# First stage of an audio tower: chunks of 512 and 480 tokens, another order of the seven products, the first norm folded into the second

## The chip, the cores and the metric

The kernel runs on one core of one Trainium2 chip. The metric is the device time of one execution in microseconds (us). Lower is better.

## The reference

```python
# x: 32 x 750 x 320, padded to 752 rows and reshaped to 32 x 94 tokens of 2560
x = rms_norm(x, ln_pre_w)                   # eps 1e-6
h = x @ w1.T                                # 1024 columns
h = silu(h[..., 512:]) * h[..., :512]
h = rms_norm(h @ w2.T, ln_post_w)           # 1024 columns, eps 1e-6
h = h + attention(layernorm(h), ...)        # 32 heads, 94 tokens per batch
h = h + ffn_with_lora(layernorm(h), ...)    # 1024 columns, 8 experts
```

All inputs and outputs are float32. There are 32 x 94 = 3008 tokens. The change is in the first four lines of arithmetic.

## The kernel before

The kernel has five parts, one behind the other: `tok_up` (w1 and the gate), `tok_down` (w2, the second norm, and products of weights for the attention), `attention`, `attn_out` and `ffn`. An fp32 product is made of three matmuls of rounded halves: each operand is split into a high half (ScalarE copies it into the rounded type) and a low half (VectorE subtracts the high half from the operand).

`tok_up` computes C = w1 x transposed: 1024 rows by 3008 tokens over 2560 inputs. It uses a scheme of seven products instead of eight: w1 and x are cut in two by two blocks, some products take a sum or difference of two blocks, and each result is added to, subtracted from or written to one or two blocks of C. `SEVEN` lists for each product the blocks of w1 (`a`), the blocks of x (`b`) and where the result goes (`into`; SET writes, NEG writes the negative, ADD adds, SUB_ subtracts, FROM writes block (0, n) less the result). The tokens are cut into six chunks (`TOKC`), two of which (one of either half) make a pair. The loop runs over 7 products x 3 pairs x 10 blocks of 128 inputs, 210 steps; ten steps with one product and pair are a group, and group(i, pr) is number 3 i + pr. A step has 4 row blocks of 3 matmuls each. The results of a group stay in four PSUM banks, and two sets of banks alternate.

For each step, SP loads one or two blocks of x (six slots `raw`, so up to three sums ahead); GpSimd adds or subtracts the two (L517, two buffers, each free when the low half of the step two sums back is made); ScalarE makes the high half (L575, five buffers t, each free when TensorE has used it); VectorE makes the low half (L668). TensorE waits for the low half (L756 is the first of the three matmuls, L758 the last). So the makers can run at most some four steps ahead of TensorE. The weights go the same way: ScalarE scales a block by the first norm's weight (L546); where the product takes a sum GpSimd adds two (L503) and ScalarE copies the high half (L558); VectorE makes the low half (L618, L621). `FILL` says at which steps of the product before, and of pair 0 of the same product (written as pair 3), the weights of a product are begun.

The first norm's factor is one number per token. During products 0 to 3 ScalarE squares each x block (L590), and the squares are added to `ssq` by VectorE (L678) where the step is a sum, and otherwise by GpSimd (L529); pair 1 of product 3 is also GpSimd's. In group(4, 1) TensorE sums `ssq` over partitions by 24 matmuls of one column in a row (L732), VectorE turns the sums into factors (L684, `inv_sqrt_wide`) and into diagonal matrices (L651), two per `RATE_AT` group. TensorE spreads them over all partitions with a matrix of ones (L739) into banks that the group itself needs for its row blocks 2 and 3, and ScalarE copies them to `ssq` (L599, L600) four steps later in its own order. VectorE then multiplies the gate half of C by the factor (L699), ScalarE takes silu, VectorE multiplies by the factor again (L703) and multiplies the value half by the gate half (L708). SP stores the result g to DRAM. VectorE evicts a group's four banks in steps 5 to 8 of the next (L639 for SET, L645 for ADD).

The last `NT` = 5 steps are done row block by row block (L770 to L772), so that VectorE can evict the first block while TensorE does the next; the last chunk's g is made and stored in four parts (L714, L495). SP waits for all stores, the stage ends, and `tok_down` loads g again in 24 tiles of 128 tokens (L904), splits w2 (L222, L229), splits g (L1027, L1124), multiplies by w2 (L244), and takes mean square, root and a Newton step for the second norm (L1059, L1149). Beside this it centres `wa` (L1235, L1109, L1001) and folds weights of the attention (L1218, L1226, L1247). Its first tiles are done by peeled code, the rest in a loop over six tiles.

## Time and profile before

| what | value |
|---|---|
| median of 3 runs | 2511.26 us (2506.93 to 2512.43) |
| profiled execution | 2511.18 us, span 2509.5 us |
| TensorE busy | 2377.4 us, 95% of the span |
| VectorE, ScalarE, GpSimd busy | 1815.0, 1246.3, 1231.2 us |
| mean granted clock of TensorE | 0.974 |
| `tok_up` | up to about 635 us |
| `tok_down` | about 635 to 960 us |

Busy time counts an engine's instructions from start to end; PE is TensorE, PEld its loads of weights, DVE VectorE, ACT ScalarE, POOL GpSimd, SP SyncE, which here only issues DMAs. The granted clock is a share of full speed, so 1.00 is 2.4 GHz and 0.50 is 1.2 GHz.

### The profile page before, as it was taken

The numbers are of one execution on the slowest core, as the hardware profiler recorded it, in microseconds if no ns is written. First come the engines' busy times: TensorE is split into PE (matmuls) and PEld (weight loads), VectorE is DVE, ScalarE is ACT, GpSimd is POOL, SyncE is SP. The second block draws the span as 40 slices with busy tenths as digits, with TensorE's granted clock in tenths as the row PEclk, the third lists the DMA queues.
The fourth block names the chain that finished last, engine by engine and source line by source line (L and its number), as shares of the span: only waits on it lengthen the run. The fifth ranks groups of instructions, "written<-read, shape, count | busy, mean of one in ns | idle before, by whom it ended". The sixth has DMA issues, their size and how long they took to land. (4 is left out here: it accounts for less than half of the span.)

```text
span 2509.5 us, 45975 instructions
## 1 busy us (share of the span) xinstructions
PE 2377.4 (95%) x14716; PEld 2061.9 (82%) x14716; DVE 1815.0 (72%) x3545; ACT 1246.3 (50%) x3736; POOL 1231.2 (49%) x1017
## 2 busy tenths in 40 slices
PE   8999999988699996999999999999999996999998
PEld 7888878776466676999999999878888885999998
DVE  8875586795446666898889898855776566777775
ACT  5664454442334545999999999922222222111110
POOL 5774675774013225677677767620676553111110
PEclk9999999999899998999999999989999998999999
DMA  7654576667556651111111111287788996211111
GB/s 251 209 175 127 183 258 226 214 227 265 165 170 198 198 188 59 48 43 56 50 55 45 51 56 54 70 284 225 213 252 244 284 288 224 71 68 68 67 67 51
DMA packets 318257, 379.44 MB, mean 151 GB/s; under 512 B 25472, under 2 KB 260480, under 8 KB 317952
## 3 DMA queue, kind: packets, MB, share of 16 engines
q1 hardware_dynamic: 310320, 349.67, 44.3%
q0 software_dynamic: 7184, 25.69, 2.6%
q10 hardware_dynamic: 576, 2.10, 0.3%
q8 instruction: 65, 1.06, 0.2%
q14 instruction: 112, 0.92, 0.1%
HBM read 295.59 MB, written 81.79 MB: 150 GB/s over the span
## 5 line engine op out<-in xcount | busy, mean ns | idle before, releaser
L1551 ACT ACTIVATE attn_prob<-attn_prob,attn_bias 94x94 f32<-94x94 f32 x1024 | 366.8, 361 | 47.3 <-DVE attn_bias L1627 46.0
L668 DVE TENSOR_TENSOR up_t_lo<-early_raw,up_t_hi 128x502 fp32r<-128x502 f32 (+1 forms) x210 | 222.1, 1060 | 142.8 <-ACT up_t_hi L575 140.6
L517 POOL TENSOR_TENSOR early_raw<-early_raw 128x502 f32<-128x502 f32 (+1 forms) x150 | 234.1, 1564 | 133.0 <-DVE up_t_lo L668 73.4
L1672 POOL TENSOR_TENSOR attn_prob<-attn_prob,attn_share 94x752 f32<-94x752 f32 x128 | 188.1, 1470 | 178.6 <-DVE attn_share L1635 178.6
L575 ACT ACTIVATE up_t_hi<-early_raw 128x502 fp32r<-128x502 f32 (+1 forms) x210 | 130.8, 623 | 281.1 <-POOL early_raw L517 158.5
L1911 POOL TENSOR_TENSOR early_raw<-early_raw 128x512 f32<-128x512 f32 x120 | 172.1, 1439 | 194.2 <-DMA early_raw<-o_t 194.0
L1946 DVE TENSOR_TENSOR out_t_lo<-early_raw,out_t_hi 128x512 fp32r<-128x512 f32 x168 | 158.5, 946 | 148.3 <-ACT out_t_hi L1925 147.5
L756 PE MATMUL up_ps<-up_t_lo,early_s_hi 128*128 128x502 f32 (+1 forms) x608 | 243.6, 401 | 18.3 <-DVE up_t_lo L668 16.1
L1925 ACT ACTIVATE out_t_hi<-early_raw 128x512 fp32r<-128x512 f32 x168 | 105.1, 631 | 302.2 <-POOL early_raw L1911 148.1
L757 PE MATMUL up_ps<-up_t_hi,early_s_lo 128*128 128x502 f32 (+1 forms) x608 | 240.5, 396 | 0.0
L758 PE MATMUL up_ps<-up_t_hi,early_s_hi 128*128 128x502 f32 (+1 forms) x608 | 239.8, 394 | 0.0
L2086 POOL TENSOR_TENSOR ffn_res<-shared_k_t,ffn_bias 128x1024 f32<-128x1024 f32 x24 | 58.6, 2445 | 314.1 <-DVE ffn_o L2208 296.4
L1551 ACT ACTIVATION_READ_ACCUMULATOR attn_prob<-attn_prob,attn_bias 94x1 f32 x1024 | 192.6, 188 | 0.0
L1606 DVE TENSOR_TENSOR attn_prob<-attn_ps_s,attn_mask 94x752 f32<-94x752 f32 x128 | 119.3, 932 | 52.5 <-PE attn_ps_s L1466 52.1
L756 PEld LDWEIGHTS up_ps<-up_t_lo,early_s_hi 128*128 128x128 f32 x608 | 116.6, 192 | 47.0 <-issue 12.1
L1969 PE MATMUL out_ps<-early_s_hi,out_t_lo 128*128 128x512 f32 x384 | 150.8, 393 | 4.4 <-DVE out_t_lo L1946 4.4
L1970 PE MATMUL out_ps<-early_s_lo,out_t_hi 128*128 128x512 f32 x384 | 150.6, 392 | 0.0
L1971 PE MATMUL out_ps<-early_s_hi,out_t_hi 128*128 128x512 f32 x384 | 150.4, 392 | 0.0
L1663 POOL TENSOR_TENSOR attn_q_a<-attn_by_cos,attn_by_sin 64x376 f32<-64x376 f32 x128 | 143.7, 1123 | 10.6 <-POOL attn_by_sin L1659 1.1
L244 PE MATMUL ffn_ps_o<-ffn_w_hi,ffn_xt_lo 128*128 128x390 f32 (+1 forms) x576 | 139.7, 350 | 8.1 <-DVE ffn_xt_lo L2174 8.1
L758 PEld LDWEIGHTS up_ps<-up_t_hi,early_s_hi 128*128 128x128 f32 x608 | 117.1, 193 | 24.7
L757 PEld LDWEIGHTS up_ps<-up_t_hi,early_s_lo 128*128 128x128 f32 x608 | 117.0, 192 | 24.3 <-issue 0.7
(261 smaller groups left out, 6697.0 us busy)
## 6 DMA issues: line engine op xcount, KB each, us to landing
early_raw<-o_t SPq DMA_DIRECT2D x288, 256.0 KB, 4.7
early_raw<-x_f SPq DMA_DIRECT2D x240, 251.0 KB, 3.6
shared_ring<-w SPq DMA_DIRECT2D x120, 256.0 KB, 3.9
early_raw<-x_f SPq DMA_DIRECT2D x120, 250.0 KB, 3.4
shared_ring<-wvo SPq DMA_DIRECT2D x96, 256.0 KB, 4.8
o_t<-attn_o_t SPq DMA_DIRECT2D x128, 188.0 KB, 1.9
shared_ring<-wo SPq DMA_DIRECT2D x32, 512.0 KB, 6.6
y<-early_raw POOLq DMA_DIRECT2D x24, 512.0 KB, 3.6
```

Of the source, the lines that this page charges most:

```text
L517: nc.gpsimd.tensor_tensor(both[n % 2][:, 0:w], a, b, SEVEN[i].op_b).then_inc(both_done, 1)
L668: nc.vector.tensor_tensor(t_lo[s % NT][:, 0:w], src, t_hi[s % NT][:, 0:w], ALU.subtract).then_inc(lo_done, 1)
L756: nc.tensor.matmul(o, sh, tl, start=(kk == 0), stop=False)
L757: nc.tensor.matmul(o, sl, th, start=False, stop=False)
L758: last = nc.tensor.matmul(o, sh, th, start=False, stop=(kk == KH - 1))
L1551: last = nc.scalar.activation(prob[u % NPR][0:SEQ, h, part], prob[u % NPR][0:SEQ, h, part], ACT.Exp, bias=bias[u % 2][0:SEQ, n:n + 1], sca ...
L1672: nc.gpsimd.tensor_tensor(p4, p4, share[u % 2][0:SEQ, :].unsqueeze(2).broadcast_to((SEQ, 8, SEQ)), ALU.mult).then_inc(prob_done, 1)
L1911: nc.gpsimd.tensor_tensor(ox.at(s), ox.at(s), ox.at(s, 1), ox.product(s).op_a).then_inc(ox.both_done, 1)
L1946: nc.vector.tensor_tensor(t_lo[s % NT][:], ox.at(s), t_hi[s % NT][:], ALU.subtract).then_inc(ox.lo_done, 1)
L1969: nc.tensor.matmul(ps[g % NB][:], t_lo[s % NT][:, j, :], sh, start=(kk == 0), stop=False)
L1970: nc.tensor.matmul(ps[g % NB][:], t_hi[s % NT][:, j, :], sl, start=False, stop=False)
L1971: last = nc.tensor.matmul(ps[g % NB][:], t_hi[s % NT][:, j, :], sh, start=False, stop=(kk == KB - 1))
```

## The change

- The chunks are 512 tokens (four) and 480 tokens (two). The sums of squares are taken per tile of 128 tokens, 24 of them with a last half filled by a constant, and the diagonals, the spread and ScalarE's copy are 512 wide, one copy instead of two.
- The order of the seven products is another: the two with a sum on the x side and one weight block are first, and all squares of products 0 and 1 are VectorE's, those of 2 and 3 GpSimd's. `FILL` begins the weights of the next product at other steps.
- The 24 one-column matmuls stand one behind each row block in the first six steps of group(4, 2), into spare columns of bank 0 of that group. The factors are made at step 154, and spread in groups (5, 1), (5, 2) and (6, 0).
- The second multiplication of the gate by the factor (L703) is gone. Since g is now too large by one over the factor, the second norm adds the first epsilon times (mean square + epsilon) of the token, `own`, in place of its own epsilon. `own` is read per tile by ScalarE's root and VectorE's scaling.
- Two steps instead of five are held back at the end.
- The first two tiles of g are copied inside SBUF from C to two slots of `raw`, and the stage's end waits for these copies and not for the stores. The load of tile 2 waits for the ten stores. The buffers of y and w2n in `tok_down` change places, small tiles move to spare columns of the ring, and three tiles of `attention` are allocated first.

```diff
-TOKC = [(0, 502), (502, 502), (1004, 502), (1506, 502), (2008, 500), (2508, 500)]
-SUB = 126
+G_STORES = 10
+TOKC = [(0, 512), (512, 512), (1024, 512), (1536, 512), (2048, 480), (2528, 480)]
+RT = 512
...
-    Product([(1, 0), (1, 1)], [(0, 0)], [(1, 0, SET), (1, 1, FROM)]),
-    Product([(0, 0), (0, 1)], [(1, 1)], [(0, 1, ADD), (0, 0, NEG)]),
-    Product([(1, 1)], [(1, 0), (0, 0)], [(1, 0, ADD), (0, 0, ADD)], minus_b=True),
+    Product([(1, 1)], [(1, 0), (0, 0)], [(1, 0, SET), (0, 0, SET)], minus_b=True),
+    Product([(1, 0), (1, 1)], [(0, 0)], [(1, 0, ADD), (1, 1, FROM)]),
+    Product([(0, 0), (0, 1)], [(1, 1)], [(0, 1, ADD), (0, 0, SUB_)]),
...
+    TAIL = 2
...
-        ssq = k_t[:, 0:TOK]
-        sq = [x[:, 0:4 * SUB] for x in ow.raw[NWR:NWR + 2]]
-        fac = mem.sb("fac", [P, KIN])
-        ones = mem.sb("ones", [P, P])
-        zero = mem.sb("zero", [P, 4, TOKP - TOK])
-        r = mem.sb("r", [P, 24])
-        var = mem.sb("var", [P, 3, 24])
+        ssq = k_t
+        sq = ow.raw[NWR:NWR + 2]
+        spare = [x[:, 2 * HID:] for x in ring]
...
-        by_pool = [s for s in adders if not is_sum(s) or place(s)[:2] == (3, 1)]
+        by_pool = [s for s in adders if not is_sum(s)]
...
-        FILL = [(2, 1), (2, 6), (2, 7), (2, 8), (2, 9), (3, 1), (3, 2), (3, 3), (3, 6), (3, 7)]
+        FILL = [(1, 9), (2, 4), (2, 6), (2, 7), (2, 8), (2, 9), (3, 1), (3, 2), (3, 3), (3, 4)]
...
-        STAT_AT = group(4, 1)
-        RATE_AT = {group(4, 2): (0, 1), group(5, 0): (2, 3), group(5, 1): (4, 5)}
-        GATE_FIRST, GATE_LAST, VALUE = {}, {}, {}
+        STAT_AT, PER = KH * group(4, 2), MB
+        assert W - width(2) >= TILES
+        STATS = ps[group(4, 2) % 2][0][:, width(2):width(2) + TILES]
+        RATE_AT = {group(5, 1): (0, 1), group(5, 2): (2, 3), group(6, 0): (4, 5)}
+        GATE_FIRST, VALUE = {}, {}
         for pr in range(PAIR):
-            GATE_FIRST[KH * group(5, pr + 1) + 0] = 2 * pr
-            GATE_LAST[KH * group(5, pr + 1) + 4] = 2 * pr
-            GATE_FIRST[KH * group(5, pr + 2) + 1] = 2 * pr + 1
-            GATE_LAST[KH * group(5, pr + 2) + 5] = 2 * pr + 1
+            GATE_FIRST[KH * group(5, pr + 2) + 0] = 2 * pr
+            GATE_FIRST[KH * group(5, pr + 2) + 3] = 2 * pr + 1
             VALUE[KH * group(5, pr + 2) + 8] = 2 * pr + 1
             if pr < 2:
                 VALUE[KH * group(6, pr + 1) + 9] = 2 * pr
...
+            sp.wait_ge(g_done, nth_value[0] + 1)
+            sp.wait_ge(both_done, len(sums) - 2)
+            for t in range(2):
+                sp.dma_start(ox.raw[t], c_t[:, 0:MB, P * t:P * t + P]).then_inc(g_early[t], 16)
...
             for m in range(MB):
                 sp.wait_ge(g_done, len(values) + m + 1)
                 sp.dma_start(d["g_t"][:, m, a:a + w], c_t[:, m, a:a + w]).then_inc(g_stored, 16)
-            sp.wait_ge(g_stored, 16 * (len(values) + 1 + MB))
+            for t in range(2):
+                sp.wait_ge(g_early[t], 16)
...
-                        bank = ps[g % 2][2 + n]
-                        nc.scalar.activation(ssq[:, a:a + 3 * SUB], bank[:, 0:3 * SUB], ACT.Copy).then_inc(rate_taken, 1)
-                        nc.scalar.activation(ssq[:, a + 3 * SUB:a + wc], bank[:, 7 * SUB - wc:4 * SUB],
+                        nc.scalar.activation(ssq[:, RT * c:RT * c + RT], ps[g % 2][2 + n][:],
                                              ACT.Copy).then_inc(rate_taken, 1)
                 if s - 2 in GATE_FIRST:
                     c = GATE_FIRST[s - 2]
...
-                if g == STAT_AT and kk == 4:
-                    dve.wait_ge(stat_made, 1)
+                if s == STAT_AT + KH + 4:
+                    dve.wait_ge(used, STAT_AT + KH)
                     link.step(0)
-                    link(nc.vector.tensor_scalar(var[0:SUB, 0, :], ps[g % 2][3][0:SUB, 0:24], 1.0 / DIN, RMS_EPS, ALU.mult,
-                                                 ALU.add))
-                    dve.sem_inc(stat_taken, 1)
-                    inv_sqrt_wide(nc, link, var[0:SUB, 0, :], var[0:SUB, 1, :], r[0:SUB, :], var[0:SUB, 2, :])
+                    link(nc.vector.tensor_scalar(var[:, 0, :], STATS, 1.0 / DIN, RMS_EPS, ALU.mult, ALU.add))
+                    inv_sqrt_wide(nc, link, var[:, 0, :], var[:, 1, :], r, var[:, 2, :])
                     link.fill()
+                    nc.vector.tensor_scalar(own, var[:, 0, :], RMS_EPS, None, ALU.mult).then_inc(own_done, 1)
...
-                if s in GATE_LAST:
-                    c = GATE_LAST[s]
-                    dve.wait_ge(silu_done, nth_gate[c] + 1)
-                    nc.vector.tensor_tensor(half(c, HIGH), half(c, HIGH), rate(c), ALU.mult).then_inc(rate_done, 1)
                 if s in VALUE:
                     c = VALUE[s]
-                    dve.wait_ge(rate_done, nth_last[c] + 1)
+                    dve.wait_ge(silu_done, nth_gate[c] + 1)
...
-                if g == STAT_AT and kk == 0:
-                    pe.wait_ge(taken, 4 * (g - 2) + 4)
+                if s == STAT_AT:
                     pe.wait_ge(sq_added, len(by_dve))
                     pe.wait_ge(sq_pooled, len(by_pool))
-                    for c, (a, wc) in enumerate(TOKC):
-                        for j in range(4):
-                            at = a + (SUB * j if j < 3 else wc - SUB)
-                            last = nc.tensor.matmul(ps[g % 2][3][0:SUB, 4 * c + j:4 * c + j + 1], ssq[:, at:at + SUB],
-                                                    ones[:, 0:1], start=True, stop=True)
-                    last.then_inc(stat_made, 1)
...
-                if s == STEPS - NT:
+                if s == STEPS - TAIL:
...
-                last.then_inc(used, 1)
+                    t = PER * (s - STAT_AT) + m
+                    if m == MB - 1:
+                        last.then_inc(used, 1)
+                    if 0 <= t < TILES:
+                        nc.tensor.matmul(STATS[:, t:t + 1], ssq[:, P * t:P * t + P], ones[:, 0:1], start=False,
+                                         stop=True, skip_group_check=True)

             for m in range(MB):
-                for s in range(STEPS - NT, STEPS):
+                for s in range(STEPS - TAIL, STEPS):
...
+        def g_of(t, u):
+
+            return ox.raw[t] if first(t, 2) else g_raw[u % 2][:]
+
         @block.sync
         def _(sp):
             def body(k, m):
                 s = stage(k, m, 0, U, TILES)
                 if s is not None:
                     t, u, kb = s
+                    if not first(t, 4):
+                        sp.wait_ge(glo_done, t - 1)
                     if not first(t, 2):
-                        sp.wait_ge(glo_done, t - 1)
-                    sp.dma_start(g_raw[u % 2][:], d["g_t"][:, :, bass.ts(t, P)]).then_inc(g_in[u % 2], 16)
+                        if first(t, 3):
+                            sp.wait_ge(g_stored, 16 * G_STORES)
+                        sp.dma_start(g_raw[u % 2][:], d["g_t"][:, :, bass.ts(t, P)]).then_inc(g_in[u % 2], 16)
...
-                    act.wait_ge(g_in[u % 2], 16 * nth(kb, u))
+                    if first(t, 2):
+                        act.wait_ge(g_early[t], 16)
+                    else:
+                        act.wait_ge(g_in[u % 2], 16 * nth(kb, u) - 16)
                     if not first(t, NG):
                         act.wait_ge(a_made, t - NG + 1)
-                    nc.scalar.activation(g_hi[u][:], g_raw[u % 2][:], ACT.Copy).then_inc(ghi_done, 1)
+                    nc.scalar.activation(g_hi[u][:], g_of(t, u), ACT.Copy).then_inc(ghi_done, 1)
...
-                    nc.scalar.activation(root[b][:, 0:1], ms[b][:, 0:1], ACT.Sqrt, bias=eps[:, 0:1]).then_inc(yroot_done, 1)
+                    nc.scalar.activation(root[b][:, 0:1], ms[b][:, 0:1], ACT.Sqrt,
+                                         bias=own[:, bass.ds(t, 1)]).then_inc(yroot_done, 1)
...
+            own = ring[2][:, 2 * HID + 64:2 * HID + 64 + TILES]
...
```

## Rows read from the trace of the kernel before

**Rows 1.** Busy time by stage: stretch, length, PE, PEld, DVE, ACT, POOL, clock, DMA, GB/s.
```profile
0.00:632.00 632.00, 600.89 (x2580) 489.67 (x2580) 470.96 (x499) 310.52 (x520) 403.28 (x273) 0.98 0.66 212
632.00:712.00 80.00, 60.35 (x213) 38.67 (x214) 31.21 (x79) 26.48 (x50) 6.49 (x15) 0.87 0.47 148
```

**Rows 2.** Waits of TensorE up to 632 us: total us, times, longest us.
```profile
PE up_ps L756 <- DVE up_t_lo L668: 19.5, 10, 8.8
PE up_ps L770 <- DVE up_t_lo L668: 8.0, 3, 2.9
```

**Rows 3.** Busy time by stretch in `tok_up`, columns as in rows 1.
```profile
64.00:91.00 27.00, 27.00 (x121) 22.39 (x120) 27.00 (x26) 19.20 (x34) 20.00 (x13) 1.00 0.69 228
91.00:118.00 27.00, 27.00 (x120) 22.33 (x119) 25.78 (x22) 20.02 (x37) 24.00 (x16) 1.00 0.68 211
311.00:339.00 28.00, 24.87 (x104) 19.50 (x104) 27.22 (x28) 18.29 (x32) 20.49 (x14) 0.97 0.66 215
339.00:371.00 32.00, 30.78 (x128) 24.30 (x128) 28.08 (x30) 17.89 (x30) 27.17 (x18) 0.97 0.87 283
504.00:531.00 27.00, 25.37 (x113) 20.71 (x111) 26.86 (x19) 13.94 (x23) 21.58 (x12) 1.00 0.63 214
531.00:560.00 29.00, 24.28 (x89) 18.79 (x90) 28.71 (x20) 15.35 (x22) 23.46 (x13) 0.88 0.78 251
```

**Rows 4.** VectorE's groups by line, 504 to 560 us: busy us, mean ns | idle.
```profile
L703 DVE TENSOR_TENSOR up_c_t<-up_c_t,shared_k_t 128x2008 f32<-128x2008 f32 (+1 forms) x4 | 11.6, 2907 | 0.0
```

**Rows 5.** Timeline: statistics, rates, small products. Start us, us, engine, line.
```profile
374.01 6.25 PE L732 MATMUL up_ps<-up_ones,shared_k_t 128*126 128x1 f32 x48
380.13 0.77 PE L756 MATMUL up_ps<-up_t_lo,early_s_hi 128*128 128x502 f32 x1
384.04 1.28 DVE L651 TENSOR_TENSOR shared_ring<-all_ident,up_r 126x504 f32<-126x504 f32 x2
...
444.10 0.47 PE L756 MATMUL up_ps<-up_t_lo,early_s_hi 128*128 128x502 f32 x1 [2.16 <-ACT shared_k_t L600]
...
675.72 0.66 PE L1218 MATMUL down_ps_f<-down_wk,down_wqn 64*128 64x64 f32 x4
```

**Rows 6.** Four lines alone: durations min/median/max in ns, starts of first and last.
```profile
L668 DVE TENSOR_TENSOR up_t_lo<-early_raw,up_t_hi x210: 661/683/1797, 8.0 to 617.8; 128x502 fp32r<-128x502 f32 x70, 128x500 fp32r<-128x500 f32 x35
L678 DVE TENSOR_TENSOR shared_k_t<-shared_k_t,shared_ring x47: 664/669/1773, 11.5 to 340.2; 128x502 f32<-128x502 f32 x28, 128x500 f32<-128x500 f32 x19
L645 DVE TENSOR_TENSOR up_c_t<-up_c_t,up_ps x84: 659/666/675, 206.6 to 630.7; 128x502 f32<-128x502 f32 x56, 128x500 f32<-128x500 f32 x28
L517 POOL TENSOR_TENSOR early_raw<-early_raw x150: 1235/1546/3274, 6.1 to 615.5; 128x502 f32<-128x502 f32 x100, 128x500 f32<-128x500 f32 x50
```

**Rows 7.** Timeline of the handover, and the last stores' time to landing.
```profile
617.36 0.79 PE L770 MATMUL up_ps<-up_t_lo,early_s_hi 128*128 128x500 f32 x1 [2.60 <-DVE up_t_lo L668]
618.40 2.24 DVE L708 TENSOR_TENSOR up_c_t<-up_c_t 128x2008 f32<-128x2008 f32 x1
630.24 0.39 PE L772 MATMUL up_ps<-up_t_hi,early_s_hi 128*128 128x500 f32 x1
631.37 0.68 DVE L714 TENSOR_TENSOR up_c_t<-up_c_t 128x500 f32<-128x500 f32 x1
635.19 0.64 SPq L904 DMA_DIRECT2D down_g_raw<-g_t  x1
643.59 1.22 PE L244 MATMUL down_ps_y<-early_s_hi,down_g_lo 128*128 128x512 f32 x2 [12.97 <-DVE down_g_lo L1124]
...
g_t<-up_c_t SPq DMA_DIRECT2D x4, 250.0 KB, 2.0
```

**Rows 8.** Timeline: start of `tok_down`.
```profile
636.18 1.06 ACT L222 ACTIVATE early_s_hi<-shared_ring 128x1024 fp32r<-128x1024 f32 x1 [18.76 <-POOL down_eps L931]
655.07 0.69 DVE L1124 TENSOR_TENSOR down_g_lo<-down_g_raw,down_g_hi 128x512 fp32r<-128x512 f32 x1 [7.78 <-ACT down_g_hi L1027]
671.35 1.97 PE L1226 MATMUL down_ps_f<-shared_ring,down_wv 128*64 128x512 f32 x4 [6.11 <-ACT down_wv_out L1016]
```

82 lines of the change are left out of this document (41 added, 41 removed).

## The prediction

> **What bounds the kernel now.** I read the stages first. In the first stage and its handover (0 to 712 us of the 2509.5 us span) TensorE is busy for 600.9 of 632 us and for 60.4 of 80 us [rows 1]; no edit changes work behind 712 us, where TensorE stays the fullest engine, so what TensorE loses before 712 us is all that can be won. The waits of TensorE come next: 19.5 us in ten waits (8.8 the first, before any x is there) for the low halves of x that VectorE makes (L668), 8.0 us in three waits for the same halves in the last five steps (L770) [rows 2]. Then I counted matmuls in stretches of about one group of ten steps. An undisturbed 27 us holds 120, which is 0.225 us each and 2.70 us for a step of twelve. From 311 to 371 us 232 were done instead of 267, so 35 x 0.225 = 7.8 us were lost; from 504 to 560 us 202 instead of 249, 47 x 0.225 = 10.6 us [rows 3]. In both places VectorE is nearly full (28.7 of 29 us in the last) and the granted clock drops to 0.97 and 0.88, because TensorE had idled. Last I read the timeline where `tok_up` ends and `tok_down` starts [rows 7, 8].
>
> **Chunks of 512 and 480.** Four chunks of 502 and two of 500 columns are 3008, as are four of 512 and two of 480. A group of widths is a pair of equal chunks, so columns per row of weights stay the same, and so do instructions per step. Cost 0. The same holds for what VectorE, ScalarE and GpSimd stream.
>
> **Order of products.** The two products with a sum on the x side and a single weight block are now first and second; the two with sums of weights and a single x follow. 54 adds of squares lie on VectorE instead of 47, and GpSimd has 60 instead of 67; the ten that go are those of product 3, pair 1, where GpSimd made the x sum and the add as well. That pair drained the lead of up to four steps (five buffers of t) that VectorE had, and the loss from 311 us on starts right behind it. Now the heavy stretch is product 1. Its third pair looks like 64 to 91 us (sums of x, squares on VectorE, weight sums of the next product begin): VectorE 27.00 of 27 us [rows 3], plus four more evictions at 0.67 us [rows 6], since product 1 now writes two blocks: 29.7, over by 2.7. The first pair of product 2 looks like 91 to 118 us, 25.8 us, plus the same 2.7: 28.5, over by 1.5. Together 4.2 us are late if no lead is left, against 7.8 now. With a full lead it is 0; with none and each step slowed as in 311 to 339 us (20 of 124 matmuls lost, 4.5 us a group) over both groups it is 9. I take 4.2, a gain of 3.6 (7.8 to -1).
> A rule of the Trainium skill speaks against this order: the page SBUF — State Buffer, section Who interferes with whom, has VectorE instructions with two SBUF inputs and GpSimd ones shut each other out entirely. The trace agrees on who is hit: L668 and L678, with two SBUF inputs, stretch from 0.66 to 1.80 us, L645, with one in PSUM, never leaves 0.66 to 0.68 [rows 6]. If the exclusion were total, product 1, pair 3 would take 10 x (0.68 + 0.67 + 1.24) + 5 x 0.68 + 6 x 1.24 = 36.7 us of the port, 9.7 too many, and the sum would end near 2493; the same load at 64 to 91 us cost TensorE nothing (121 matmuls) and took less than 5 us of the lead.
>
> **Statistics between matmuls.** The burst of 24 one-column products (48 records) fills 374.01 to 380.13 us, the first matmul behind it shows 0.77 us, and some twelve are 0.42 us apart instead of 0.225, since the clock fell: 6.1 + 12 x 0.19 = 8.4 us [rows 5]. Now each of the 24 stands behind three long matmuls. Nothing in the trace is just this. From below: 0.255 each as in the burst, 6.1 us. From above: two small fp32 products among long ones (L1218, four records) take 0.66 us [rows 5], 0.33 each, and with 0.07 for uncovered weights 0.4, 9.6 us. I take 0.3, nearer to the second row, since the weights of the next long matmul are uncovered in both: 7.2 us, without a fall of the clock. Gain 1.2 (2.3 to -1.2). TensorE no longer waits there; the chain of 13 small VectorE instructions (3.7 us, up to 384.04) and two diagonals (1.28 us) [rows 5] moves behind the group and takes lead instead.
>
> **Rates and gates.** Six multiplications L703 of 2.9 us go, 17.4 us of VectorE [rows 4]. In steps 171 to 186, where the loss of 10.6 us arises after a lead of some 8 us is used up, eight multiplications stood, and four stay, with two diagonals of 0.65 us moved in. That is 4 x 2.9 - 1.3 = 10.3 us less. What is 18.6 us of lead and loss becomes 8.3, about the lead. But the rates are now copied at steps 164, 174 and 184, and TensorE may not pass its third row block before ScalarE copied them; that was 2.16 us once, at 444.10, with 7 us of lead [rows 5] (the lead is the start of a step on TensorE less the end of its L668). At group (6,0) the lead will be near 5, so I price this wait at 4; at (5,1), behind the statistics, at 2.5; at (5,2) at 1. Now 10.6 + 2.2 = 12.8, afterwards 7.5: gain 5.3. Bounds: 0, if the lead is gone at step 180 just the same, and 11. The new bias `own[:, t]` and its copy on VectorE stand in a loop; should they need an instruction for the address, 24 times at most 0.15 us, the smallest VectorE row there, bounds it at 3.6; TensorE hides it and I take 0.
>
> **The last steps.** Today TensorE takes the last five steps row block by row block, so it needs all five before the second block: 8.0 us idle before three of them [rows 2], 2.60 of it before 617.36, and after VectorE finished the low half of the last step (618.40) it still has 45 matmuls to do, until 630.24 + 0.23 [rows 7]. With two steps held back, steps 205 to 207 are done in full as they come: step 207 from 617.36 to 620.1, then 24 matmuls, 5.4 us: 625.5. When the loads arrive doesn't change (same bytes, same queue order). Gain 5.0; with half of these at the low clock, 3.
>
> **The handover.** VectorE's last product then ends about 627.1 instead of 632.05. Today SP waits for the stores of g (2.0 us from issue to landing [rows 7]) and the next stage's first load is issued at 635.19. Now SP waits for two copies inside SBUF, issued behind a store of 1 MB and the zeros at 620.7: issue near 622, with what is ahead 1.6 MB, from 621 on at the 283 GB/s of 339 to 371 us [rows 3] until 627, 2 us to land, 629. The stage ends near 629.5, 5.7 us earlier than now, the 5.0 of the last steps in it (bounds: 3 and 7).
> Behind it TensorE starts at 643.59, 8.4 us after 635.19, because the first g tile lands late. With the tile there, the chain is ScalarE L222 (at +1.0 for 1.06 [rows 8]), the high half 0.63, VectorE's split of w2 and the low half until +4.0: 4.4 us won. The second tile also landed late: its low half at 655.07 held back the evictions of tile 0, queued behind it on VectorE, for 3.6 us, and these end in the wait of 6.11 us before 671.35 [rows 8]. Followed through with the tile present (column means directly behind tile 0, 4.9 us; tile 1 5.8; norms; centring 3.8; squares and root 2.7) that wait ends at +29 instead of +36.2: 7.0 us in all, 4.4 of them sure. Late next is tile 2, whose load waits for ten stores; it would land at about +20.5, before VectorE reaches it at +20.2 to 21, so I hold nothing for it.
>
> **Sum.** 3.6 + 1.2 + 5.3 + 5.7 + 7.0 = 22.8 us. The profiled execution took 2511.18 us, 1.7 more than its span, and the median of the runs is 2511.26: 2488 us.
>
> **Rivals.** (a) The lead never runs out: products 1 and 2 cost nothing (4.2 more) and the rates nothing but their matmuls (6 more): 2478. For it: 64 to 118 us, most like the new stretch, has 241 matmuls in 54 us, no loss; against: VectorE at 27.00 of 27. 0.20. (b) The handover gives less: the copies of 512-byte rows queue behind the 1 MB store, or tile 2 and the weights of the folding land last: 6 us less, 2494. For it: g's loads took 7 us in this crowd. 0.16. (c) The lead is gone at step 180 as now and the copies of the rates wait at full price, about 9 us: 2496. 0.12. (d) The other side: in product 1 sums, squares and low halves collide at every step. At the largest durations, 1.80 + 1.77 + 0.5 for evictions, VectorE needs 4.1 us against 2.70; over 30 steps that is 41 us, less the 4.2 counted: 2525, slower. It decides from a mean of L668 plus L678 of 3.0 us. Against: in 64 to 91 us nothing was lost. 0.05. (e) The stalls only change place and the handover is bound by loads: within 0.2%. 0.02. The forecast, 2482 to 2494, has 0.45.
>
> Range 2475 to 2500: it takes in (a) to (c) and leaves out (d), (e) and the far ends. Within 0.2%, 5 us, nothing can be told from no change: 0.03. Slower 0.05, faster 0.92.
>
> **What would show it.** Right: 120 matmuls in every 27 us from 311 to 371 us; one stretch of some 6 to 9 us shared by rates and gates; the last up matmul about 5 us after the last low half starts to be used; the first down matmul 4 us after the stage's start, and no wait over 5 us before the folding. Wrong: a loss near 150 to 190 us (product 1, pair 3), waits for ScalarE's rate copies above 5 us each, or SP still waiting for DMAs when VectorE has ended.

## The result and the profile after

| kernel | runs | median, us | range, us |
|---|---|---|---|
| before | 4 | 2510.66 | 2506.93 to 2512.43 |
| changed | 4 | 2467.87 | 2465.68 to 2469.25 |

The ratio is 0.983, 95% interval 0.9814 to 0.9845: 42.8 us faster where 22.8 were forecast. 2467.87 lies below the range of 2475 to 2500. The direction was right, the size was not.

First the stages of the changed kernel, from the busy time by stretch (columns as in rows 1; the borders are 32 us earlier, since the first stage now ends at 603 us).

```profile
0.00:600.00 600.00, 578.63 (x2580) 482.51 (x2580) 462.27 (x500) 309.73 (x514) 391.44 (x267) 0.99 0.69 223
600.00:680.00 80.00, 66.25 (x241) 43.74 (x241) 35.08 (x87) 27.55 (x53) 7.42 (x15) 0.91 0.54 175
```

The same 2520 long matmuls take 22 us less busy time than in rows 1 (600.89 to 578.63). Busy time was no term of the forecast. So matmuls became shorter, and not only waits: some by their width, some because fewer of them ran at the low clock (mean 0.99 instead of 0.98); the experiments take this apart. Then the waits of TensorE in that stage (total, times, longest):

```profile
PE up_ps L745 <- DVE up_t_lo L671: 10.8, 3, 10.1
PE up_ps L745 <- ACT shared_k_t L605: 10.3, 1, 10.3
PE down_ps_y L244 <- DVE down_g_lo L1129: 7.2, 1, 7.2
```

Of rows 2 nothing is left but the first wait before any x is there (10.1 us now) and two of 0.4 us. The 8.0 us in the last steps are gone. One new wait of 10.3 us has come, for a copy of rates on ScalarE. By stretch, those that answer to rows 3:

```profile
64.00:91.00 27.00, 27.00 (x126) 23.25 (x125) 26.71 (x31) 15.50 (x29) 16.32 (x12) 1.00 0.86 276
173.00:200.00 27.00, 26.23 (x114) 20.85 (x113) 26.96 (x25) 18.54 (x33) 24.63 (x16) 1.00 0.60 181
309.00:335.00 26.00, 26.00 (x121) 22.47 (x120) 18.94 (x22) 18.67 (x33) 21.30 (x16) 1.00 0.54 181
335.00:363.00 28.00, 28.00 (x125) 23.03 (x124) 21.55 (x23) 12.16 (x20) 21.38 (x15) 1.00 0.75 234
504.00:531.00 27.00, 16.66 (x62) 12.68 (x61) 20.75 (x17) 15.11 (x22) 20.10 (x12) 0.81 0.75 249
531.00:560.00 29.00, 29.00 (x129) 24.03 (x128) 23.08 (x20) 9.75 (x13) 17.60 (x11) 1.00 0.72 236
```

At 64 to 91 us 126 matmuls stand where 121 stood. At 309 to 363 us nothing is lost, as forecast, and VectorE is busy for 40.5 of 54 us, not full. At 173 to 200 us VectorE is full (26.96), the new heavy stretch. At 504 to 531 us 62 matmuls were done and the granted clock is 0.81: the new wait, and slow matmuls behind it. The timeline rows for the statistics, the rates, the last matmul of the stage and the handover (start, us, engine, line; idle time and its releaser in brackets):

```profile
390.59 0.28 PE L752 MATMUL up_ps<-shared_ring,shared_k_t 128*128 128x1 f32 x2
...
516.16 0.63 ACT L583 ACTIVATE up_t_hi<-early_raw 128x512 fp32r<-128x512 f32 x1 [3.23 <-POOL early_raw L525]
516.70 1.32 ACT L554 ACTIVATE shared_ring<-shared_ring 128x512 f32<-128x512 f32 x2
517.93 1.06 ACT L605 ACTIVATE shared_k_t<-up_ps 128x512 f32<-128x512 f32 x2
518.64 0.76 PE L745 MATMUL up_ps<-up_t_lo,early_s_hi 128*128 128x512 f32 x1 [10.34 <-ACT shared_k_t L605]
...
599.42 0.38 PE L766 MATMUL up_ps<-up_t_hi,early_s_hi 128*128 128x480 f32 x1
603.08 0.34 SPq L908 DMA_DIRECT2D down_post<-post_ln  x1
607.04 1.22 PE L244 MATMUL down_ps_y<-early_s_hi,down_g_lo 128*128 128x512 f32 x2 [7.24 <-DVE down_g_lo L1129]
633.27 1.98 PE L1231 MATMUL down_ps_f<-shared_ring,down_wv 128*64 128x512 f32 x4 [4.77 <-ACT down_wv_out L1017]
```

To see where 42 us went I cut every profiled execution at the same matmuls. The table is not a view; it is worked out from the starts of the matmuls in the timeline. Step n begins with matmul 12n of the first stage; "last" is the stage's last matmul, "down" the first of the second stage, "attn" the first of attention. Each column is the time between two marks, us.

```
                    start  0-105 105-130 130-150 150-180 180-205 205-last last-down down-attn | attn at
before                8.8  289.2    82.1    59.9    86.5    79.5     24.3      13.4     318.2 | 961.8
changed              10.1  285.8    66.9    58.4    85.2    80.3     12.8       7.6     311.8 | 918.9
changed again         9.1  285.1    66.8    58.4    85.2    81.0     12.8       7.5     314.6 | 920.5
e1  widths alone      8.9  285.7    85.8    58.6    88.8    79.9     24.4      13.0     320.2 | 965.2
e1b padded rows       8.8  285.2    84.1    59.6    85.5    79.0     25.2      13.2     316.0 | 956.5
e3  tail 2 alone      8.6  289.6    80.9    59.2    89.9    79.3     16.3      14.6     313.8 | 952.2
e12 loop head         9.0  288.9    82.3    59.5    86.7    79.4     23.5      13.1     309.0 | 951.3
e9  old widths        9.9  289.8    68.3    59.9    86.7    80.9     13.3       7.3     313.9 | 930.0
e9b old, padded       9.1  285.6    67.4    59.0    85.2    79.4     13.4       8.2     314.3 | 921.5
e4  old order         8.8  285.1    76.9    58.4    85.2    76.7     12.8       9.6     319.9 | 933.2
e5  second gate      10.0  284.7    66.9    58.4    87.4    83.7     13.4      10.0     312.6 | 926.9
e2  tail 5            9.1  285.6    66.8    58.4    85.2    79.8     15.4       7.3     311.5 | 919.1
e6  g from DRAM      10.1  284.8    66.8    58.4    85.2    79.5     12.8      10.4     313.6 | 921.5
e8  rates earlier    11.1  284.1    66.8    58.4    85.2    70.7     18.1       8.4     310.0 | 912.9
e10 loop head 0       8.9  285.9    66.8    58.4    85.8    78.2     12.8       8.6     312.9 | 918.4
e11 loop head 128    10.4  285.5    66.8    58.4    85.2    81.0     12.8       7.2     312.3 | 919.6
e13 rates, wa        10.3  285.0    66.8    58.4    85.2    71.0     12.8      10.1     310.5 | 910.0
e14 e13 + e10         9.0  285.4    66.8    58.4    85.2    71.7     13.1      10.4     310.4 | 910.5
e15 copies first     10.7  285.4    66.8    58.4    85.2    71.2     13.0       8.5     308.7 | 907.9
```

The first two rows differ by 42.9 us at the first attention matmul, and from there to the end of the span by 0.7 the other way. How much moves by itself: between the two profiles of the changed kernel 1.0 us at the start, up to 0.8 in a column of the first stage, 2.8 in the second stage. Runs whose edit lies elsewhere show more: e10, edited in the second stage only, has 78.2 at 180-205 (80.3 and 81.0 in the changed kernel), and e3, edited in the last steps only, 89.9 at 150-180 (86.5 before). So one profile carries a difference of 2 to 3 us in a column only where the trace also shows its cause.

### The profile page after: what moved, and what is told of

It reads as the page before. It is cut to its first block and busy times, and to the rows that moved or that the text cites. A ratio compares the mean times of both kernels' runs of the same rounds, so it can differ in the third digit from the quotient of the medians.

```text
span 2467.2 us, 46001 instructions
## 1 busy us (share of the span) xinstructions
PE 2349.8 (95%) x14716; PEld 2050.8 (83%) x14716; DVE 1809.8 (73%) x3547; ACT 1246.0 (51%) x3730; POOL 1219.1 (49%) x1011
## 5 line engine op out<-in xcount | busy, mean ns | idle before, releaser
L671 DVE TENSOR_TENSOR up_t_lo<-early_raw,up_t_hi 128x512 fp32r<-128x512 f32 (+1 forms) x210 | 221.1, 1057 | 122.7 <-ACT up_t_hi L583 121.1
L525 POOL TENSOR_TENSOR early_raw<-early_raw 128x512 f32<-128x512 f32 (+1 forms) x150 | 227.6, 1521 | 143.6 <-DMA early_raw<-x_f 79.4
L583 ACT ACTIVATE up_t_hi<-early_raw 128x512 fp32r<-128x512 f32 (+1 forms) x210 | 130.8, 623 | 262.2 <-POOL early_raw L525 138.3
L745 PE MATMUL up_ps<-up_t_lo,early_s_hi 128*128 128x512 f32 (+1 forms) x616 | 241.9, 393 | 21.2 <-DVE up_t_lo L671 10.8
L746 PE MATMUL up_ps<-up_t_hi,early_s_lo 128*128 128x512 f32 (+1 forms) x616 | 238.9, 388 | 0.0
L747 PE MATMUL up_ps<-up_t_hi,early_s_hi 128*128 128x512 f32 (+1 forms) x616 | 238.8, 388 | 0.0
L1668 POOL TENSOR_TENSOR attn_q_a<-attn_by_cos,attn_by_sin 64x376 f32<-64x376 f32 x128 | 144.3, 1128 | 10.6 <-POOL attn_by_sin L1664 1.1
```

The costliest lines, as they stand in the source:

```text
L525: nc.gpsimd.tensor_tensor(both[n % 2][:, 0:w], a, b, SEVEN[i].op_b).then_inc(both_done, 1)
L671: nc.vector.tensor_tensor(t_lo[s % NT][:, 0:w], src, t_hi[s % NT][:, 0:w], ALU.subtract).then_inc(lo_done, 1)
L745: nc.tensor.matmul(o, sh, tl, start=(kk == 0), stop=False)
L746: nc.tensor.matmul(o, sl, th, start=False, stop=False)
L747: last = nc.tensor.matmul(o, sh, th, start=False, stop=(kk == KH - 1))
```

## Experiments

Times are medians; "ratio" is to the kernel before, run on the same chip. The changed kernel stands at 0.983 (first time) and 0.9826 (again, below). Its runs and those of an experiment were mostly on different chips, so between two kernels the ratios are compared first; 0.001 is 2.5 us. "Spacing" is the time from the start of one long matmul to the start of the next at the full clock.

**e1, the widths alone.** In the kernel before:

```
-TOKC = [(0, 502), (502, 502), (1004, 502), (1506, 502), (2008, 500), (2508, 500)]
-SUB = 126
+TOKC = [(0, 512), (512, 512), (1024, 512), (1536, 512), (2048, 480), (2528, 480)]
+SUB = 128
...
-    W = 502
+    W = 512
```

> The kernel before with only the chunks changed: 512 and 480 columns instead of 502 and 500, tiles of x padded to 512 elements, row pieces of the statistics 128 wide; product order, burst of statistics, gates, last steps and handover as before. Theory A (columns of matmuls do not cost what their number says: 0.2285 us at 502, 0.2261 at 500, 0.2267 at 512, 0.2167 at 480): 1680 x (0.2285 - 0.2267) + 840 x (0.2261 - 0.2167) = 3.0 + 7.9, so 9 to 11 us less than before, nearly all of it in the third pair of each product. Theory B (the prediction's step, equal columns per row of weights cost the same): within 2 us of before.

2508.1 us, ratio 0.9994 (0.9982 to 1.0005): no difference, as theory B had it. But the matmuls did become shorter: their mean spacing is 0.2272 and 0.2167 us. The table resolves the two: 3.5 us are gained up to step 105, and more than that is lost at 105 to 130 (85.8 instead of 82.1) and 150 to 180 (88.8 instead of 86.5). Those stretches are set by VectorE, whose work is the same, so faster matmuls only use up its lead sooner; and the deeper idle time lowers the granted clock (0.97 before, 0.95 here, third number from the right):

```profile
298.00:380.10 82.10, 77.75 (x349) 63.10 (x349) 64.48 (x70) 42.09 (x71) 64.01 (x43) 0.97 0.75 240
```
```profile
294.50:380.30 85.80, 78.43 (x349) 64.46 (x349) 64.86 (x71) 42.07 (x72) 63.82 (x44) 0.95 0.72 234
```

(first the kernel before, then e1, each between steps 105 and 130; VectorE is busy for 64.5 and 64.9 us). The cost of 0 was right for the step alone and wrong for the step in the company of the others.

**e9, the old widths inside the changed kernel.**

```
-    W = 512
+    W = 502
...
-        STATS = ps[group(4, 2) % 2][0][:, width(2):width(2) + TILES]
+        STATS = [ps[group(4, 2) % 2][x][:, width(2):width(2) + TILES // 2] for x in range(2)]
```

with the old `TOKC`.

> The changed kernel with the chunks of before (502 and 500 columns, tiles of x with rows of 502 elements); the 24 columns of the statistics stand in two banks, twelve in each, since 500 columns leave only twelve free. All else as changed. Theory E (the widths are worth nothing alone, since VectorE sets the pace wherever TensorE's lead is gone, and their full price once order, gates and statistics have freed VectorE): 9 to 11 us slower than the changed kernel, with spacings of 0.2285 and 0.226 us and a lead that stays above 3 us behind step 185. Theory B (the prediction's: equal columns cost the same): within 2 us of the changed kernel, as the widths alone moved the kernel before by 1 us.

2478.88 us, ratio 0.9857 (0.9838 to 0.9876). The last up matmul comes at 608.80 instead of 599.42 us. By the table 4.0 + 1.4 + 1.5 + 1.5 + 0.6 + 0.5 = 9.5 us, in every column of the stage: theory E. Spacings are 0.2283 and 0.2264 us at 502 and 500 columns, 0.2269 and 0.2166 at 512 and 480 in the changed kernel: 1680 x 0.0014 + 840 x 0.0098 = 10.6 us. With VectorE's load gone TensorE sets the pace nearly everywhere, and the widths are worth 9.5 us of the stage. The whole time is 7 to 8 us longer by the ratios, 11 by the medians.

**e1b and e9b, rows padded, widths old.** Only `W = 512` in the kernel before, and e9 with `W = 512`. A row is the piece of a tile of x that lies on one partition; the tiles stand one behind the other, so with rows of 502 elements they start 2008 bytes apart, with rows of 512 elements 2048.

> The kernel before with only the tiles of x (and their halves) padded from 502 to 512 elements a row, chunks still 502 and 500 wide. Theory A1 (502 and 500 columns are slow because the tiles start at addresses that are no round multiple): spacings fall from 0.2285 and 0.2261 towards 502 and 500 over 512 of 0.2267, that is 0.222 us, and some 10 us go. Theory A2 (the number of columns itself does it): spacings and time stay, within 2 us.

> The changed kernel with chunks of 502 and 500 columns in tiles of 512 elements a row; the statistics in two banks. Of the 9.4 us that the old widths with rows of 502 elements cost in the first stage (last up matmul), the padding gives back 1680 x (0.2284 - 0.2235), 8 us: the last up matmul within 2 us of the changed kernel's. Against it: if padding only shows where VectorE reads x too, less than 3 us of the 9.4 come back.

e1b: 2503.25 us, ratio 0.9982 (0.9969 to 0.9995), 1 to 8 us less. Spacing of the 502-column matmuls 0.2234 us instead of 0.2282, of the 500-column ones 0.2258 instead of 0.2264. This is theory A1 for 502 columns and A2 for 500. e9b: the last up matmul at 599.00, 0.4 us ahead of the changed kernel's (0.6 behind, counted from the first matmul on), so in the first stage the padding alone gives back nearly all of the 9.4 us. In rows of 512 the spacing goes nearly by the columns: 0.2234 x 512/502 is 0.2278 and 0.2258 x 480/500 is 0.2168, where the changed kernel has 0.2269 and 0.2166. The prediction's rule would have held there; the tiles of 502 elements broke it.
The whole time of e9b does not show this gain: 2474.89 us at 0.9856 (0.9834 to 0.9879), the same ratio as e9, some 6 us more than the reading allows. Its profiled execution took 6.3 us longer than the changed kernel's first, 0.6 us of it in the first stage, 3.1 in the handover and second stage and 3.6 behind them, where no edit reaches (less 1.0 at the start); this stays unexplained. So the padding is shown by the traces of the first stage, not by the time of the kernel.

**e7, the matmuls alone.**

```
+CASES = [(512, 512), (502, 512), (502, 502), (500, 512), (500, 502), (480, 512), (496, 512), (504, 512), (508, 512),
+         (510, 512), (506, 512), (494, 512), (512, 512)]
...
+            for n, (w, st) in enumerate(CASES):
```

> Matmuls alone: 13 cases of 108 matmuls in the pattern of the first stage (128 x 128 weights, fp32r, four banks in turn), with the moving operand's tiles apart by 512 or 502 elements; nothing of the reference is computed and no other engine works beside them. Columns and distance of tiles, in order: 512/512, 502/512, 502/502, 500/512, 500/502, 480/512, 496/512, 504/512, 508/512, 510/512, 506/512, 494/512, 512/512. Theory A3 (the matmul itself is slow where rows of 2008 bytes put its operand off a round address, or where the number of columns is no multiple of 16 or 32): 0.2267 us at 512, 0.2167 at 480, 0.2235 at 502/512 and 0.2285 at 502/502, as in the whole kernels. Theory A4 (the difference comes from the other engines' traffic to the same memory): 502/502 and 502/512 have the same spacing here, below that of 512.

The first matmul of each case in the timeline; a case is 108 matmuls, so the spacing is the difference of two starts over 108.

```profile
39.59 0.39 PE L2344 MATMUL all_ps<-all_tl,all_wh 128*128 128x502 f32 x1
63.71 0.39 PE L2344 MATMUL all_ps<-all_tl,all_wh 128*128 128x502 f32 x1
88.43 0.39 PE L2344 MATMUL all_ps<-all_tl,all_wh 128*128 128x500 f32 x1
112.91 0.39 PE L2344 MATMUL all_ps<-all_tl,all_wh 128*128 128x500 f32 x1
137.47 0.39 PE L2344 MATMUL all_ps<-all_tl,all_wh 128*128 128x480 f32 x1
160.89 0.39 PE L2344 MATMUL all_ps<-all_tl,all_wh 128*128 128x496 f32 x1
```

502 columns in rows of 512: (63.71 - 39.59) / 108 = 0.2233 us. 502 in rows of 502: (88.43 - 63.71) / 108 = 0.2289. 500: 0.2267 in rows of 512, 0.2274 in rows of 502. 480: 0.2169. From the same timeline 0.2234 at 496 and 494, 0.2266 to 0.2277 at 504, 506, 508, 510 and 512 (the second time; the first meets the low clock). With no other engine at work these are nearly the spacings of the whole kernels: theory A3, and A4 (traffic) falls. Of A3's two causes the same trace points at the start of the tile. The case of 502 in rows of 502 uses five tiles in turn. The first starts where it does in rows of 512, and its matmuls are 0.2235 us apart (0.2233 in rows of 512); those of the other four, whose starts are shifted, are 0.2270 to 0.2457 apart. Being a multiple of 16 does not decide: 494 is as fast as 496. Why 502 columns are faster than 500 in padded rows stays open.
The Trainium skill (TensorE: Matmul & The Clock Gate, section "Wait — 56ns, not 53.3ns?") gives, for back-to-back matmuls, N over 2.4 GHz plus some 2.5 ns between starts, 215.7 ns at N = 512. Here, where each matmul comes with new weights, 226.7 ns at 512 and 216.9 at 480 were measured (e7), and steps in place of a straight line. The measurement decides.

**e4, the old order of products**, its loading plan and its share of adds, in the changed kernel.

> The changed kernel with the order of products of before, its loading plan and its share of adds on GpSimd (product 3, pair 1 again adds there), 512 and 480 columns. By the prediction's step 3.6 us slower than the changed kernel; by the trace of the changed kernel, which lost about 1 us where 7.7 were lost before, 6 to 8 us slower; and by theory F (with faster matmuls VectorE binds in the old heavy stretch, so part of the widths' gain goes there too) 9 to 12 us slower, with the stretch of steps 105 to 130 taking about 82 us minus the burst, as in the kernel before.

2483.4 us, ratio 0.988 (0.9862 to 0.9898), 12 to 15 us slower than the changed kernel, more than any of the expectations. Between steps 105 and 130 it takes 76.9 us, the changed one 66.9: 10.0 us, theory F for this stretch. The two rows (e4 first, then changed) show what differs. VectorE carries 60.1 us in the one and 45.7 in the other, and GpSimd 59.5 against 49.9:

```profile
293.90:370.70 76.80, 69.60 (x301) 55.41 (x300) 60.12 (x68) 40.23 (x69) 59.54 (x40) 1.00 0.73 236
```
```profile
295.80:362.80 67.00, 67.00 (x302) 56.24 (x301) 45.67 (x51) 38.25 (x65) 49.90 (x36) 1.00 0.66 209
```

3.6 us come back at 180 to 205, where its wait for the rates is 6.7 us instead of 10.3, so from the first to the last up matmul the old order costs 5.7 us net. From the last up to the first down matmul it is 2.0 us longer, and the second stage takes 319.9 us instead of 311.8, though no edit touches it. e10 to e12 show where that comes from.

**e5, the second multiplication of the gates back.**

```
+        GATE_LAST = {x + 4: c for x, c in GATE_FIRST.items()}
...
+                    nc.vector.tensor_tensor(half(c, HIGH), half(c, HIGH), rate(c), ALU.mult).then_inc(rate_done, 1)
```

> The changed kernel with the second multiplication of each gate by its rate on VectorE put back, six instructions of 2.9 us, four steps behind the first one (each gate is so scaled by its rate twice, which the changed kernel leaves to the second norm). By the prediction's step (lead and loss of 10.3 us less in the rates' stretch, 5.3 of it time) 4 to 7 us slower. Theory G (the changed kernel's lead of 8.9 us behind step 185 comes from the wait of 10.3 us for the rate copies, which is there anyway and gives VectorE the same time back): the six fit into wait and lead, less than 3 us slower, and the lead at step 205 falls to about 2 us.

2475.83 us, ratio 0.985 (0.9831 to 0.987), 5 to 8 us slower. In the first stage 2.2 + 3.4 + 0.6 = 6.2 us, inside the prediction's 4 to 7. Theory G falls: the wait for the rates did not swallow them, it grew from 10.3 to 13.8 us, and the lead at step 205 is 7.2 us, not 2. That the wait grew because ScalarE's queue in front of the copy waits for the gates is a guess; it was not tried apart.

**e2 and e3, the last steps.**

```
-    TAIL = 2
+    TAIL = 5
```
```
-                if s == STEPS - NT:
+                if s == STEPS - 2:
...
-                for s in range(STEPS - NT, STEPS):
+                for s in range(STEPS - 2, STEPS):
```

> The changed kernel with the last five steps taken row block by row block again, instead of the last two. Theory C (the last steps are fast because fewer are held back): the idle time of TensorE before them comes back, 5 to 8 us slower than the changed kernel. Theory D (they are fast because VectorE enters them with a lead of 8.9 us, three steps, against 2.7 before): all five low halves are there within 3 us of the first of them, so nothing waits and the time stays within 1 us.

> The kernel before with only the last two steps held back instead of five. By the prediction's step 5.0 us less than before (3 if half of the matmuls meet the low clock). Theory D (the lead is what counts, and here it is 2.7 us): VectorE ends no earlier, TensorE only fills its waiting time with matmuls, so it gains between 3 and 5 and TensorE's remaining waits in the last five steps add up to 3 us or more.

e2: 2469.12 us, ratio 0.9842 (0.9825 to 0.986), 205-last 15.4 instead of 12.8 us. e3: 2503.62 us, ratio 0.9973 (0.996 to 0.9987), 205-last 16.3 instead of 24.3. So in that column the shorter tail is worth 8.0 us in the kernel before, where the lead at step 205 is 2.7 us, and 2.6 us where it is 8.9. Of the 8.0 us 1.2 are given back up to the first down matmul (14.6 instead of 13.4), and the whole time is 5.5 us less by the medians, 3 to 10 by the ratio. e3's gain in the column is above both expectations (5.0, and 3 to 5); its remaining waits in the last steps are 2.0 us. e2's time is 1.3 us above the changed kernel's by the medians and 3 to 4 by the ratios, with intervals that overlap. That is between theories C and D: the lead makes the tail's form worth about a third, not nothing.

**e6, g from DRAM.**

```
-            for t in range(2):
-                sp.dma_start(ox.raw[t], c_t[:, 0:MB, P * t:P * t + P]).then_inc(g_early[t], 16)
...
+            sp.wait_ge(g_stored, 16 * G_STORES)
+            for t in range(2):
+                sp.dma_start(ox.raw[t], d["g_t"][:, :, P * t:P * t + P]).then_inc(g_early[t], 16)
```

> The changed kernel without the two copies of g inside SBUF: SP waits for all stores of g again, and tiles 0 and 1 are loaded from DRAM right behind that wait, into the same buffers. By the prediction's steps 7.0 us slower in the handover and about 1 more for the stage's end, 6 to 8 in all, with the first down matmul 8 us behind the stage's start instead of 4. Theory H (the loads of g only shift, the wait before the folding is set by other loads): the first down matmul is late by 4 to 5 us, and that is all, 4 to 5 us slower.

2475.33 us, ratio 0.9848 (0.9832 to 0.9865). From the last up to the first down matmul 10.4 us instead of 7.6 (13.4 before). By the ratios that is 4.5 to 5.5 us slower than the changed kernel. In the handover neither expectation holds: the first down matmul stands 3.96 us behind SP's next issue all the same, because the loads were issued 2.6 us ahead of it, under the stage's end. So 2.8 us of the 5.8 belong to the copies; the other 3.0 (13.4 to 10.4) come with the tiles from DRAM too, presumably from issuing them before the stage's end; that was not tried apart. The second stage is 1.8 us longer in the one profile; that is within what it moves by itself.

**The anchor, and e10 and e11, VectorE's loop in the second stage.**

```
-            run_steps(dve, TILES, DEPTH, U, step)
+            run_steps(dve, TILES, DEPTH, U, step, at=0)
```

(128 in e11.)

> The changed kernel itself once more, as the anchor for the others of this chip: a ratio to the kernel before of 0.983, and a first attention matmul some 311.8 us behind the first down matmul.

> The changed kernel with the head of VectorE's loop in the second stage loaded at slot 0 of a block of instructions; nothing computed is changed. Theory K (the idle time of VectorE at each return of that loop, 5.5 to 6.6 us in the kernel before and 4.2 to 4.3 in the changed one, comes from where the loop's instructions lie): it is another number here, and the time from the first down to the first attention matmul moves by two to three times the difference. Theory L (it comes from what VectorE waits for): the two gaps stay at 4.2 to 4.3 us and the time stays within 1 us.

> As the run with the loop's head at slot 0, with slot 128. Theory K: the gap at the loop's return differs from both the changed kernel's 4.2 us and that of slot 0, by up to 3 us; theory L: 4.2 to 4.3 us again.

The anchor is the changed kernel once more: 2468.06 us, ratio 0.9826 (0.9806 to 0.9846). e10: 2464.14, ratio 0.9817 (0.9797 to 0.9837); e11: 2464.23, ratio 0.9815 (0.9796 to 0.9834). Both lie within the anchor's interval, so their times alone show nothing. In the timeline VectorE's first instruction of each new round of that loop waits for nothing that the profile shows; the rows of the kernel before, of the changed one and of e4:

```profile
802.52 0.69 DVE L1124 TENSOR_TENSOR down_g_lo<-down_g_raw,down_g_hi 128x512 fp32r<-128x512 f32 x1 [5.54 <-issue]
870.50 0.69 DVE L1124 TENSOR_TENSOR down_g_lo<-down_g_raw,down_g_hi 128x512 fp32r<-128x512 f32 x1 [6.26 <-issue]
```
```profile
763.75 0.69 DVE L1129 TENSOR_TENSOR down_g_lo<-down_g_raw,down_g_hi 128x512 fp32r<-128x512 f32 x1 [4.19 <-issue]
829.96 0.69 DVE L1129 TENSOR_TENSOR down_g_lo<-down_g_raw,down_g_hi 128x512 fp32r<-128x512 f32 x1 [4.32 <-issue]
```
```profile
774.80 0.69 DVE L1131 TENSOR_TENSOR down_g_lo<-down_g_raw,down_g_hi 128x512 fp32r<-128x512 f32 x1 [6.09 <-issue]
844.35 0.69 DVE L1131 TENSOR_TENSOR down_g_lo<-down_g_raw,down_g_hi 128x512 fp32r<-128x512 f32 x1 [5.94 <-issue]
```

The gap was 3.3 us in e5 and 6.0 and 6.6 in e1. It depends on the kernel, and between runs of one kernel it moves by up to 0.6 us (4.78 and 4.37 in the anchor). With a fixed head both are gone (in e10 one of 3.2 us stands where the loop is entered), and with them the two waits of TensorE for ScalarE (1.2 and 1.3 us). From TensorE's wait for `wga_lo` to its first wait for `down_qk` (both in every kernel) it takes 236.1 us in e10 and in e11, 237.9 and 238.6 in the two profiles of the changed kernel, 243.3 before, 244.7 in e4, and 235.9 in e5 with its gaps of 3.3 us. From the first down matmul to attention e10 and e11 show no gain (312.9 and 312.3, against 311.8 and 314.6), since this column moves by 2.8 us by itself.

**e12, the same in the kernel before.**

> The kernel before with the head of VectorE's loop in the second stage loaded at slot 0 of a block of instructions, nothing else changed. Theory K (of the 6.4 us by which the second stage is shorter in the changed kernel some 5 come from where this loop's instructions happen to lie, no edit of the change): the two gaps of VectorE of 5.5 and 6.3 us fall below 2 us, as they did with fixed heads in the changed kernel, ScalarE's part of them that TensorE waits for (2.5 and 3.2 us) goes, and 5 to 7 us less than before. Theory L (the gap is idle time that costs nothing, or is filled by another wait): within 2 us of before.

2500.58 us, ratio 0.997 (0.9956 to 0.9984), 4 to 11 us less; the second stage takes 309.0 us instead of 318.2. Where VectorE waited over this stretch (the two returns in it), in e12 and then in the changed kernel:

```profile
DVE down_z L1142 <- PE down_ps_y L244: 16.0, 10, 3.4
DVE down_vec L1159 <- ACT down_root L1068: 5.8, 11, 0.6
```
```profile
DVE down_g_lo L1129 <- issue: 8.5, 2, 4.3
DVE down_z L1147 <- PE down_ps_y L244: 7.3, 6, 3.3
```

No issue gap is left at these two returns in e12 (VectorE waits for TensorE instead; one of 2.8 us stands where the loop is entered). Theory K. Between the two marks above e12 takes 235.3 us, so with the head fixed in both kernels the change gains nothing in this stretch, and its 5 us there (243.3 to 237.9) are no edit's doing: they come with where the loop happened to lie. The times agree: the fixed head gives 7.5 us before (0.997) and 2 to 4 in the changed kernel. So about 5 of the 42.8 us are luck.
The Trainium skill (Runtime: NRT & Kernel Launch, section "Instruction fetch mechanics") says that a taken branch whose target is not among the instructions held must fetch it first. The trace agrees in this: the gap stands at the returns of the loop (with a head at slot 0 once at its entry), and it goes when the head is placed. What the engine does in the gap no run here shows.

**e8, e13, e14, e15, a better version.** e8 lets ScalarE copy the last two rates two steps earlier; e13 also moves the load of wa; e14 adds the fixed loop head; e15 issues the early copies of g ahead of the last store of 1 MB.

```
-                if g in RATE_AT and kk == 4:
+                if g in RATE_AT and kk == (2 if g == group(6, 0) else 4):
```
```
-                if s == STEPS - 5:
-                    sp.wait_ge(gate_scaled, len(TOKC))
-                    sp.dma_start(k_t[:].rearrange("p (n w) -> p n w", n=KM), d["wa"]).then_inc(wa_in, 16)
...
+            sp.wait_ge(gate_scaled, len(TOKC))
+            sp.dma_start(k_t[:].rearrange("p (n w) -> p n w", n=KM), d["wa"]).then_inc(wa_in, 16)
```

> The changed kernel with ScalarE's copies of the last two rates put behind its high half of step 182 instead of 184 (the other four copies stay where they are). Theory I (the wait of 10.34 us at 518.64 is the place of this copy in ScalarE's order: it stands behind a gate's Silu, two scalings and a high half that waits for a sum on GpSimd): the copies run near 508.5, the wait falls to 2 to 4 us, VectorE then has less lead behind it, and 5 to 8 us of the 10.3 are gained. Theory J (VectorE is full from 499 to 520 us and would be late anyway): the wait turns into waits for low halves, under 2 us gained.

> The changed kernel with the last two rates copied two steps earlier (which alone gave 4.0 us) and with the load of the 1.5 MB of wa moved from five steps before the end to behind the early copies of g. Theory M (the last five steps are held by the x tiles that arrive behind wa and stores, as GpSimd's waits of 2.5 to 4 us for them show; 18.1 us from step 205 to the last matmul, where 13.0 are the matmuls): 3 to 5 us less than the run with earlier rates alone, with the last up matmul 13 to 14 us behind step 205. Theory N (VectorE's evictions and gates hold them, or the stores do): within 1 us of that run, or slower where the column means now wait for wa in the second stage.

> The changed kernel with three edits that were run apart: the last two rates copied two steps earlier (4.0 us), wa loaded behind the early copies of g (about 2), and the head of VectorE's loop of the second stage at slot 0 (about 2 between the folding and the end of that stage). If they add up: 8 us less than the changed kernel, a ratio to the kernel before of 0.9795. If the moved load of wa gives its gain back in the handover (SP issued the next stage's first load 5.9 us behind the last up matmul instead of 3.7), 6 us.

> As the three together, and the two early copies of g issued ahead of the last 1 MB store instead of behind it. Theory O (the stage's end waits for these copies, which land behind the store): SP issues the next stage's first load 3.5 to 4 us behind the last up matmul instead of 5.9, and 2 us go. Theory P (the end is set by VectorE's last product and SP's last issues): 5.9 stays, within 1 us of the three together.

e8: 2464.1 us, ratio 0.9819 (0.9801 to 0.9837). ScalarE's copies in its timeline, now between a scaling and the gate's Silu:

```profile
507.44 1.06 ACT L605 ACTIVATE shared_k_t<-up_ps 128x512 f32<-128x512 f32 x2
508.39 1.91 ACT L610 ACTIVATE up_c_t<-up_c_t 128x2048 f32<-128x2048 f32 x1
```

The wait fell from 10.3 to 0.6 us and steps 180 to 205 from 80.3 to 70.7, 9.6 us: theory I. But the last five steps went from 12.8 to 18.1 us, so 5.3 were given back: the wait had also given VectorE its lead of 8.9 us (now 2.1 at step 205). By its ratio the whole time gains 2 to 3 us, within the intervals. What stands behind it there are GpSimd's waits for x in the last steps, before, in e8 and in e13:

```profile
POOL early_raw L517 <- DMA early_raw<-x_f: 12.5, 4, 4.8
```
```profile
POOL early_raw L525 <- DMA early_raw<-x_f: 9.1, 3, 4.0
```
```profile
POOL early_raw L524 <- DMA early_raw<-x_f: 4.9, 2, 2.5
```

With wa moved (e13: 2462.03 us, ratio 0.9821, 0.9802 to 0.9841) the last five steps take 12.8 us again: theory M in place. But the next stage is issued 5.9 us behind the last matmul instead of 4.4, so 2 us of it are given back, and by its ratio the whole time is that of e8 (0.9821 and 0.9819): theory M is shown by the column, its 3 to 5 us are not in the time. e14: 2462.14 us, ratio 0.9811 (0.9794 to 0.9828), 910.5 us at attention as in e13, so the fixed head shows nothing there; of the 8 us expected the time shows 6 by the medians and 4 to 5 by the ratios. e15: 2456.35 us, ratio 0.9795 (0.9778 to 0.9811); the stage's end comes 4.3 us behind the last matmul instead of 6.3: theory O. It beats the kernel before by 50 us on its chip, and the changed kernel by 8 to 9 us by the ratios and 12 by the medians. It is the only one of these versions that its interval sets apart from the changed kernel's first (0.9814 to 0.9845), and it overlaps the second (0.9806 to 0.9846).

## Why the prediction was wrong

In the prediction's order, forecast and measured gain, us. Measured is from the table, with the widths' share taken out by e9. Each entry is from one profile of each kernel and good to 1 to 3 us.

```
term                                     forecast   measured
widths                                        0        9.5   (9.4 at the last up matmul, e9)
order of products and burst             3.6 + 1.2      8.6   (13.8 at 105-130, less 5.2 for the new statistics)
rates and gates                               5.3      3.6   (130-205: 2.0, + 5.2 statistics, - 3.6 widths)
last steps                                    5.0     11.0   (11.5 less 0.5 widths)
from the last up to the first down matmul     5.1      5.8
second stage                                  2.6      6.4
start, rest of 0-105, behind attention          0     -2.5   (-1.2, -0.6, -0.7)
sum                                          22.8     42.4   (the spans, 2509.5 and 2467.2: 42.3)
```

- **Chunks of 512 and 480: the step that failed.** "Columns per row of weights stay the same" took the time of a matmul as its columns times a constant. I took one number, 0.225 us, for all widths, from counting 120 matmuls in 27 us. The trace of before had the spacings to hold against each other: 0.2282 us at 502 columns, 0.2264 at 500, and 0.2267 at 512 in the matmuls of `attn_out` (L1969), so ten columns more cost less. In place of 0 the widths were worth 9.5 us (e9). What was slow was a tile of x that starts at a multiple of 2008 bytes: padding alone gives the first stage the same time (e9b), and e7 shows it in the matmuls alone. e1 shows why trying the widths alone would not have found it.
- **Order of products: right in place, mis-sized.** No loss from 311 to 371 us, and some 1 us at 187 to 191, where I had named the risk at 150 to 190: 0.35 and 0.41 us of waiting, not 4.2. But the load was not smaller than forecast, it was twice as large: the lead fell from 9.0 us at step 50 to 1.1 at 60 and 0.1 at 65. In pair 3 of product 1 that is 7.9 us, where I had 2.7 (and 9.7 for total exclusion, which this does not prove). It cost next to nothing only because the lead was full at its start, and none of it was left at the end; this part is luck. Undoing the order costs 10.0 us in its stretch now (e4) and 5.7 net in the stage; that this is more than 3.6 because faster matmuls hit a full VectorE harder is argued, not shown.
- **Statistics: right, the cost was too high.** Row 390.59 is one one-column product (two records) in 0.28 us; the first matmuls of the row blocks before and behind it stand 0.87 us apart instead of 3 x 0.2167, so 0.22 each and 5.2 in all, not 7.2, without a fall of the clock. At 105 to 130 e1 takes 8.9 us more than e4; 6.1 of it are the burst, the rest was not taken apart.
- **Rates and gates: the work priced right, the wait wrong.** e5 gives 6.2 for the six multiplications. The copy of group (6, 0) cost 10.3 us, priced at 4 and named as a rival at 9; it was not VectorE's lead that set it, but the place in ScalarE's order behind a Silu, two scalings and a high half that waits for a sum (516.16 above): two steps earlier in that order 0.6 us is left (e8).
- **Last steps: mis-sized, and coupled.** 5.0 was taken from 45 matmuls that fill the idle time. e3 gives 8.0 for that alone in its column and 5.5 in the whole time; with the lead that the wait for the rates leaves, the idle time vanishes and 11.0 are gained. So part of this gain is paid for by that wait. e8 and e13 show that x behind wa and stores is what is late there when the lead is small.
- **Handover: right.** 4.0 us from the stage's start to the first down matmul, as worked out; the shift of its end, 0.7 beside the tail, was 1.3. The wait before the folding was to end 29 us behind SP's first issue and ends at 30.2 (603.08 to 633.27).
- **Second stage: 1.5 of the 2.6 came** (the folding stands 26.2 instead of 27.8 us behind the first down matmul); the other 4.9 are the loop's place, which no step had (e12).

Rival (a), that the lead never runs out, was the nearest with 2478, and held for products 1 and 2; (c)'s wait of 9 us came true beside it. The range left no room for terms costed at nothing.

## What to carry to other kernels

Read the spacing of matmuls by shape before costing a change of shape: a few per cent on 2520 matmuls outweighed nearly every wait that I had counted, and in the first stage padding the rows alone gives the same. A saving on one engine may show only once the other engine that paces the same stretch is free (the widths: 1 us alone, 9.5 in company), so price terms together; and a wait removed in one place may have been the lead of the next. When a stage changes that no edit touches, look at the first instruction behind each loop's return before looking for a cause in the work.

## What was not expected of the hardware

- fp32r matmuls of 128 x 128 weights, spacing at the full clock: 0.2169 us at 480 columns, 0.2234 at 494 and 496, 0.2233 at 502 in rows of 512 elements but 0.2289 in rows of 502 (0.2235 on the tile whose start is not shifted, 0.2270 to 0.2457 on the other four), 0.2266 to 0.2277 from 504 to 512 and at 500 (e7).
- A one-column fp32 product between long matmuls costs 0.22 us (changed kernel, 390 to 394 us), as much as a whole 480-column one.
- At each return of VectorE's loop stand from nothing (e10, e11, e12) to 6.6 us (e1) of idle time; placing the head removes it, with nothing else in the kernel changed.
